# Moving one of four key-window copies per block from ScalarE to VectorE in a fused attention and channel-mix kernel

## The reference

```python
q = (x @ Wq + bq)   # 16 heads of 16, in 4 groups
k = (x @ Wk + bk)   # 4 heads of 16
v = (x @ Wv + bv)
scores = einsum(q, k) / sqrt(16)
mask = (i - 128 >= j) | (i < j)          # a query sees itself and the 127 keys before it
att = softmax(where(mask, -1e9, scores))
x = layernorm(x + (att @ v) @ Wo + bo)

x_prev = x moved by one token
xr = mu_r * x + (1 - mu_r) * x_prev ;  xk = mu_k * x + (1 - mu_k) * x_prev
r = sigmoid(xr @ W_r.T) ;  k_act = square(relu(xk @ W_k.T))
x = layernorm(x + r * (k_act @ W_v.T))
```

## Time and profile before

| | |
|---|---|
| three runs | 399.24, 397.92, 398.92 us, median 398.92 |
| the profiled execution | 400.57 us, its span 398.8 us |
| PE busy | 369.7 us (93%), 2333 instructions |
| PE weight loads | 230.7 us (58%) |
| ACT busy | 341.7 us (86%), 701 instructions |
| DVE busy | 331.9 us (83%), 859 instructions |
| POOL busy | 288.4 us (72%), 484 instructions |
| L682, the window copies on ACT | 128 of 727 ns, 89.4 us busy |
| the chain that ended last | PE 63%, ACT 19%, DMA 7% |

### The profile page before, as it was taken

How to read it: one execution, slowest core, us unless ns; L and a number is a source line. 1 busy time by engine, 2 the same in 40 slices (tenths; PEclk the granted TensorE clock), 3 DMA queues, 4 the chain that set the end, 5 groups by cost and what they waited for, 6 DMA issues and landing times.

```text
span 398.8 us, 8155 instructions
## 1 busy us (share of the span) xinstructions
PE 369.7 (93%) x2333; PEld 230.7 (58%) x2334; DVE 331.9 (83%) x859; ACT 341.7 (86%) x701; POOL 288.4 (72%) x484
## 2 busy tenths in 40 slices
PE   6874699999999999999999999999999998998984
PEld 3442245666666666566666666666565666665562
DVE  8277477799899988999899989999899998997654
ACT  3358499999999999999999999999999998986743
POOL 5124366987689876888788868887699777778633
PEclk9997599999999999999999999999999999999988
DMA  7386438542576328732864437622854253000001
GB/s 285 118 182 142 90 94 174 124 80 54 97 179 90 88 47 162 163 68 54 124 163 85 100 66 177 124 53 55 133 135 80 72 90 58 16 15 17 26 15 39
DMA packets 51292, 39.24 MB, mean 98 GB/s; under 512 B 33712, under 2 KB 42928, under 8 KB 51120
## 3 DMA queue, kind: packets, MB, share of 16 engines
q1 hardware_dynamic: 50288, 35.18, 42.1%
q10 hardware_dynamic: 960, 3.54, 2.5%
HBM read 26.38 MB, written 12.06 MB: 96 GB/s over the span
## 4 chain that ended last, share of the span: by engine, by line
PE 63%; ACT 19%; DMA 7%; issue 4%; SPq 3%; DVE 3%; POOL 1%; POOLq 0%; DVEq 0%; ACTq 0%
PE av_ps L1287 14%; PE score_ps L1270 10%; PE gen L1306 8%; PE gen L1377 7%; PE proj_ps L1190 6%; PE max_ps L1251 5%; ACT probs L663 5%; PE gen L1364 3%; ACT windows L682 3%; PE gen L1347 3%; DMA x_t<-x_feat 2%; ACT x L702 2%; DMA qs<-q_parts 2%; ACT out_t L740 2%; PE av_ps L1322 2%
## 5 line engine op out<-in xcount | busy, mean ns | idle before, releaser
L485 POOL TENSOR_SCALAR_AFFINE_SELECT probs<-probs 128x512 f32<-128x512 f32 x252 | 164.2, 668 | 56.9 <-ACT probs L663 54.9
L663 ACT ACTIVATE probs<-score_ps 128x512 f32<-128x512 f32 x252 | 142.7, 593 | 18.0 <-PE score_ps L1270 17.1
L939 DVE TENSOR_REDUCE neg_max<-max_ps 128x3 f32<-128x480 f32 x146 | 88.7, 631 | 15.5 <-PE max_ps L1251 15.2
L1270 PE MATMUL score_ps<-qs,ks 98*128 98x512 bf16 x252 | 88.7, 392 | 5.6 <-DMA qs<-max_rows 3.5
L682 ACT COPY windows<-ks 96x640 bf16<-96x640 bf16 x128 | 89.4, 727 | 4.0 <-DMA ks<-k_parts 3.0
L1287 PE MATMUL av_ps<-probs,vals 128*32 128x512 f32 x488 | 59.9, 606 | 0.0
L980 DVE SCALAR_TENSOR_TENSOR mix<-diff,first,x_t 128x128 f32<-128x128 f32 x128 | 52.8, 455 | 2.9 <-POOL diff L513 2.6
L1251 PE MATMUL max_ps<-windows,q_tiles 128*128 128x160 bf16 x420 | 50.8, 237 | 3.7 <-DVE neg_max L939 2.2
L1251 PEld LDWEIGHTS max_ps<-windows,q_tiles 128*128 128x128 bf16 x420 | 36.1, 99 | 23.9 <-issue 4.8
L1270 PEld LDWEIGHTS score_ps<-qs,ks 98*128 98x128 bf16 x252 | 21.4, 98 | 41.5 <-issue 28.0
L492 POOL TENSOR_TENSOR rstd<-var,minus_half 128x1 f32<-128x1 f32 x64 | 35.4, 554 | 10.6 <-DVE var L963 10.4
(11 more groups left out here) (112 smaller groups left out, 617.0 us busy)
## 6 DMA issues: line engine op xcount, KB each, us to landing
q_parts<-parts SPq DMA_DIRECT2D x42, 128.0 KB, 2.2
out<-out_t SPq DMA_DIRECT2D x32, 128.0 KB, 2.3
qs<-q_parts SPq DMA_DIRECT2D x7, 576.0 KB, 6.8
ks<-k_parts SPq DMA_DIRECT2D x42, 80.0 KB, 3.3
qs<-q_parts SPq DMA_DIRECT2D x8, 384.0 KB, 8.2
x_t<-x_feat SPq DMA_DIRECT2D x6, 512.0 KB, 9.1
x_in<-x_nat SPq DMA_DIRECT2D x6, 512.0 KB, 3.8
qs<-q_parts SPq DMA_DIRECT2D x15, 192.0 KB, 3.3
```

The lines of the kernel that those rows point to most:

```text
L485: nc.gpsimd.affine_select(out=v, in_=v, compare_op=ALU.is_ge if i % 2 else ALU.is_gt, fill=0.0, base=0, pattern=[[0, HPG], [sign, BLK]], c ...
L663: nc.scalar.activation(probs[:, buf, i], score_ps[i % 2][:, :], ACT.Exp, scale=SCALE).then_inc(s_exp, 1)
L939: nc.vector.tensor_reduce(neg_max[:, TPB * i:TPB * i + n], max_bank(t, j, i)[:, 0:n * TILE_KEYS].rearrange("p (n k) -> p n k", k=TILE_KEYS ...
L1270: nc.tensor.matmul(score_ps[i % 2][:, :].rearrange("p (h q) -> p h q", q=BLK), ks[0:ROWS + MPARTS, par, g, k0:k0 + BLK], qs[0:ROWS + MPART ...
```

## The change

The copy for the last group of heads (half = 3, one of four per block) leaves ACT's queue, where it stood behind exps(t, 5), and goes to DVE's queue as last_windows, behind tile_q and ahead of normalise. It counts on a semaphore of its own, s_window_v; ACT's count per block falls from four to three, and PE waits for both. The access pattern moves into a function that both use. DVE's copy takes the waits for the keys that ACT's first copy had: in the start, and where j = 0.

```diff
+        def sliding(par, j, g, n):
+            src = ks[0:ROWS, par, g:g + n, j * BLK:j * BLK + TILE_KEYS]
+            (lanes, rows), (g_step, _), (k_step, _) = src.ap
+            return bass.AP(src.tensor, src.offset,
+                           [[lanes, rows], [g_step, n], [k_step * SUB, NSUB], [k_step, TILE_KEYS]])
...
-                window_copy(0, 0, 0, 0, 3)
...
-                window_copy(1, 0, 1, 0, 3)
...
-                if more:
-                    window_copy(t + 2, s2, j2, p2, 3)
...
+            def last_windows(t, s, j, par):
+                if t == 0:
+                    dve.wait_ge(s_zero, 1)
+                    dve.wait_ge(h_stack_k, K_STACKS)
+                elif t == 1 or j == 0:
+                    dve.wait_ge(s_stack_k, s * K_STACKS + K_STACKS)
+                g = GROUPS - 1
+                nc.vector.tensor_copy(windows[0:ROWS, j % 2, g:], sliding(par, j, g, 1)).then_inc(s_window_v, 1)
...
                 if maxima and (project or j < SB_BLKS - 2):
                     tile_q(t + 2, s if j < SB_BLKS - 2 else s + 1, *at(j, par, 2))
+                    last_windows(t + 2, s if j < SB_BLKS - 2 else s + 1, *at(j, par, 2))
...
-                    pe.wait_ge(s_window, (t + 1) * WINDOW_OPS)
+                    pe.wait_ge(s_window, (t + 1) * (WINDOW_OPS - 1))
+                    pe.wait_ge(s_window_v, t + 1)
```

More of the change, by code:

```diff
@@ L198, in attention_channel_mix @@
         s_window = sem("s_window")
+        s_window_v = sem("s_window_v")
         s_maxsc = sem("s_maxsc")
@@ L677, in window_copy @@
                 g, n = GROUPS // WINDOW_OPS * half, GROUPS // WINDOW_OPS
[L678 to L682, removed]
+                nc.scalar.copy(windows[0:ROWS, j % 2, g:g + n], sliding(par, j, g, n)).then_inc(s_window, 1)
             def att_t_copy(u):
@@ L1072, in start @@
                 tile_q(0, 0, 0, 0)
+                last_windows(0, 0, 0, 0)
                 tile_max(0, 0, 0)
@@ L1082, in start @@
                 tile_q(1, 0, 1, 0)
+                last_windows(1, 0, 1, 0)
                 rest_part(1, 2, av_ps)
```

## The result

The changed kernel takes **406.36 us** (median of 5 runs, 405.4 to 408.65), the kernel before 398.92 beside it (397.92 to 399.77). The ratio is 1.0198, with a 95% interval of 1.0162 to 1.0235: slower by 7.4 us between the medians, 7.9 by the ratio. The forecast was 409.6, between 400 and 416. One execution of a later run (VectorE's part alone) took 534.38 us at a granted clock of 0.65 and is left out. The profiled execution took 408.65 us, its span is 406.9; the one before took 400.57, so the profiles differ by 8.1.

What follows compares the result with a forecast made beforehand. PE, ACT and DVE were all taken as nearly full, 43.8 us a superblock. Start -0.5, loop +10.1 and end +1.1 gave +10.7 us on 398.92, so 409.6 us, range 400.0 to 416.0.

Steps and rivals of the forecast that it cites:

- Part 1: ACT's queue behind exps(t,5): losing one copy per block gains PE at most 0.65 us a superblock.
- Part 2: DVE's queue behind tile_q: the added copy per block has a bare length of 0.20 us.
- Part 3: DVE behind tile_q: the copy waits for a POOL mask, making att 0.72 us late and all that follows 0.67.
- The loop: Superblocks in the middle: 2.73 us delay less 0.96 filled gives 1.77 each; six, less 0.5 in the first, give +10.1.
- Start, -0.5: Before the loop: one ACT copy fewer gives 0.65 us, of which DVE's copy may take 0.2 back.
- End, +1.1: Last three blocks that copy windows: 0.67 us late each, partly filled by short waits; the least certain term.
- Which waits could be filled: DVE's waits per superblock: 0.65 us in j=0 and j=1 can be filled, 1.0 and 0.25 in j=3 can't.
- POOL lets the copy through: DVE behind tile_q: the copy asks ahead of the mask in every block and costs 0.20 us; 396.5 us, chance 0.11.
- Column by column: DVE's copy runs slowly, 0.76 us a block, and leaves POOL alone; 411.3 us, chance 0.07.
- L999 catches the earlier boundary: second_residual's final operation goes ahead of the third mask, so only att is late, by 0.72 us; 400.1 us, chance 0.10.
- q_tiles blocked too: DVE in j=1 and j=2: the query tiles' copy also meets a started mask, 0.5 us more each; 415.6 us, chance 0.12.

Runs made afterwards that it cites:

- VectorE's part alone: Kernel before, ScalarE keeping all four copies, with VectorE also copying the last quarter for blocks 2 to 31 into an unread buffer: 405.85 us, ratio 1.0173.
- the last run: Kernel before with the start alone changed, VectorE copying the last quarter of the first two blocks: 397.31 us, ratio 0.9962.
- the unlocked operation: Changed kernel with VectorE's copies for blocks 2 to 31 replaced by an about equally long maximum over a constant: 397.14 us, ratio 0.9957 to the kernel before.
- the short masks: Both kernels with three of GpSimd's seven masks a block cut short: kernel before 397.95 us, changed kernel 395.69 us, faster than its partner by 2.3 us.
- e9: Changed kernel with the last quarter of the first two blocks copied by ScalarE at the start: 404.88 us, ratio 1.0155 to the kernel before.
- e4: Changed kernel with VectorE's copy moved behind att and ahead of second_residual: 403.86 us, ratio 1.0130 to the kernel before.

## Why the prediction was right, and where its terms were off

- **Time and sign.** 406.36 for 409.6. In the profiles +8.1 for +10.7.
- **Part 1, ScalarE's relief, at most 0.65 us a superblock on PE.** Right as a bound: 0.2 in the run of it alone (43.58 for 43.82). Of that run's 2.9 us, the start alone gives 1.5 by the last run; the rest is the loop, 1.2 us over five superblocks in the profiles.
- **Part 2, bare length 0.20.** 0.20 ahead of the query tiles, 0.24 behind them.
- **Part 3, the wait behind the masks.** Right in its place and size: att is late by 0.67 (1.52 for 0.85) where the text said 0.72, the statistics of second_residual by 0.67 (2.71 for 2.04) where it said 0.67, and the sum's 0.82 stayed. PE meets this as the text said: in the superblock from 240.88 on it waits once for att (0.5 us, at the end of j=2), and its other listed waits are short ones for later products of DVE's queue (rest, neg_max). The new copy's median of 0.754 and shortest of 0.314 are close to the 0.75 and 0.28 named. The loss is gone in both runs without that wait (the unlocked operation in the copy's place, 397.14, and the short masks, -2.3 us).
- **The loop.** 45.57 was forecast for four waiting copies; the superblock from 104.28 to 149.92 has just that, and takes 45.64. The next, where q_tiles waited once as well, takes 46.08, and those where j=1's copy is let through 44.9. The text called j=1 and j=2 a toss for themselves and had both waiting, and j=0 for certain. j=2 was always blocked, j=1 was let through in the late superblocks, and in the first loop both j=0 and j=1 were. That is the step that made the sum too large: at the first projection chunk of the sixth j=3 the profile is 6.85 us behind (285.74 for 278.89), and with the last of the six loops some 7.4, for 10.1. The first loop cost 0.6, for 1.27; two copies let through, at 0.44 us each, are in that.
- **Start, -0.5.** 0 in the profile (first chunk of j=3 at 60.71 for 60.69), -1.5 in the timed runs of the start alone. That the estimate lies between the two is luck: it knew nothing of a copy that takes 1.28 us in some executions.
- **End, +1.1.** The rest of the profiles' difference, some 0.7.
- **Which waits could be filled.** DVE's in j=0 and j=1 went; the 0.9 and 0.2 in j=3 stayed, as forecast, and PE's wait for att appeared ahead of its turn.
- **The rivals.** "POOL lets the copy through" holds for single places, not as a state. Its price (396.5) assumed that a bare copy in this row costs next to nothing. The unlocked operation bears that out nearly (397.14), the bare copy ahead of the query tiles does not (403.39): what is free depends on whether the added operation shifts the moment at which the masks start. "Column by column" fell with the shortest record, 0.31 us, "L999 catches the earlier boundary" with the 0.82 throughout, and "q_tiles blocked too" came true in one block of the loops (1.14).

What stays open: how the loss divides between late att and the longer group, which no run separates in the changed kernel's order; which event in the first 30 us decides the start's course, and whether the lower time of the run with the start on ScalarE (e9) is more than chance.

## What to carry to other kernels

Before a copy is moved to VectorE, look at what GpSimd has queued at that very place: here an operation that gives way held the queue for 0.67 us, most of it the neighbour's, where its own length is 0.2, and an operation of equal length that doesn't give way cost too little, beside ScalarE's relief, to make the kernel slower. In a row where everything waits at fixed boundaries, ask for each added piece whether it only eats into a later wait or shifts the boundaries themselves, and then check each consumer of the row apart (here att, the spans and the query tiles each had PE waiting once they were last). Where no gap of the engine is as long as the piece, leave it where it is; a busy share of 83 against 86% says nothing about that.

## What the runs showed of the hardware

- The copy of 640 bf16 columns per partition out of overlapping spans of 256 takes 0.28 us behind a transpose and 0.31 behind another copy, a third of the 0.84 of first_mask, 640 columns from f32. So overlapping source rows don't bring it down to that pace; no copy of this size without overlap ran beside it.
- A VectorE record includes the time in which it gives way: 0.28 to 0.32 bare, mostly 0.72 to 0.79 behind a mask, 1.28 behind a parts operation of POOL. The record's length so tells what POOL was running.
- VectorE's tensor_reduce over f32 in SBUF was 270 to 278 ns in 30 of 30 places beside running masks, where the copy in the same place took 0.75 in most blocks.
- Two operations that give way and stand next to each other can share one wait: behind att (e4) the copy took 0.73 and then the sum 0.41, while the next mask, whose record starts at 238.30, inside the copy's, took 1.06 us for 0.63. Elsewhere (q_tiles, then the copy) the mask that asked during the first went in between the two. What decides between these isn't shown.
